# A stack of graph and expert layers on one core: late rotations folded inside the batch rounds, with rows made by GpSimd

## The chip, the cores and the metric

The kernel runs on one core of one Trainium2 chip. The metric is device time in microseconds (us) of one execution. A core has TensorE (PE; its weight loads stand apart as PEld), VectorE (DVE), ScalarE (ACT), GpSimd (POOL), SyncE (SP), which here only issues transfers, and 16 DMA engines that all queues share. Each engine works off its own instructions in order, and the engines meet at semaphores.

## What is computed

Eight layers follow one another on 6250 nodes of 256 values, with 100,000 edges. The change lies in the first. It builds a 256x256 matrix from plane rotations, one an edge, applied in the order of the edges, and multiplies the normalised nodes by it:

```python
def _build_mat(rots, idx_i, idx_j, ndim):
    def step(mat, t):
        i, j, theta = t
        c, s = jnp.cos(theta), jnp.sin(theta)
        ri, rj = mat[i], mat[j]
        mat = mat.at[i].set(c * ri - s * rj)
        mat = mat.at[j].set(s * ri + c * rj)
        return (mat, None)
    mat, _ = jax.lax.scan(step, jnp.eye(ndim), (idx_i, idx_j, rots))
    return mat.T
...
x = x + _layernorm(x) @ _build_mat(edge_weight, src, dst, 256)
```

The rotation's i is the edge's source and j its destination. The edges are sorted by destination and their numbers run to 6249, while the matrix has 256 rows; a read past the end gives the last row, a write past it does nothing.

## The kernel before

The kernel is a row of phases. A phase (`Phase`) holds a block with one program for each engine and ends when all engines have come to its end. The first phases are `constants`, `rotations`, `layernorm_stats` and `x_plus_product`, and the expert layer follows.

`constants` makes an identity and a row of column numbers, and SyncE loads the whole of x into `g.x`; the phase ends when x is in.

`rotations` builds the matrix `m`. An edge whose destination is below 256 is *early*: it changes two rows. An edge whose destination is higher but whose source is below 256 is *late*: it only scales row i and adds a multiple of the last row to it. The phase goes through these steps.

1. SyncE loads sources, destinations and weights. DVE counts the early edges, prepares their event records, and POOL scatters the records to DRAM (`steps`) with 40 indirect DMAs. Then SyncE writes a padding behind them (L2911).
2. DVE makes a record for each late edge (`rec`, stored by ScalarE as `late_records`) and lists, for each of 128 partitions, the late edges it holds (`keys`, then `edge`), in passes of eight. At L3138 the list is done.
3. The batches (L3147 to L3175). 64 events make a batch. SyncE loads a batch's events (`own`, `around`); DVE works out which event feeds which (L3151 to L3166) and releases the load of the next batch; TensorE squares that matrix six times (`powers`), with a copy by ScalarE between; at each of the six levels DVE adds TensorE's product `p_t` to `t` (L3170). TensorE then turns `t` and multiplies it by `m` (ScalarE copies twice), and DVE updates `m` (L3173, L3174).
4. POOL fetches, while the batches run, the late records of each partition's list: it copies 56 indices (L2957) and issues 56 indirect DMAs (L2961), each of which brings one record of four numbers to each partition (`got`).
5. The folds (L3179 to L3187). DVE takes the records one after another. For each it makes two one-hot rows of 256 (L3183, L3184: column number equal to the source, times a factor), and folds them into the pair `ab` with two more instructions (L3185, L3186).
6. The tail. TensorE turns `ab`, DVE multiplies the partitions' pairs together and applies them to `m`, and TensorE turns the result into `g.mt`.
7. ScalarE, at the end of its program, issues 21 large writes that fill and clear tables of later layers (`inject8`, `inject4`, and in `clear_first` `expert_rows` and `back`); the first expert layer waits for them by `g.filled`.

`layernorm_stats` then has DVE go over the 49 tiles of x for mean and variance, and `x_plus_product` starts with ScalarE's normalising of the first tile.

All four numbers that set the loops (blocks of early edges, batches, units of late edges, events) are counted by the kernel in `sizes` and loaded into registers. No planner is at work: the order on each engine is the order of the code.

## Time and profile before

| | us |
|---|---|
| median of 3 runs | 8275.56 (8267.13 to 8279.29) |
| profiled execution, its time | 8263.3 |
| its span, first to last instruction | 8261.1 |
| busy in the span: PE, DVE, ACT, POOL | 5259.0, 3680.5, 3299.8, 4671.5 |

The profile is of one execution, and times in its rows count from the start of the span. A row of a timeline gives start, duration, engine, line, operation, output and inputs, and in brackets how long the engine stood idle before it and what released it. "q" behind an engine's name means its instruction queue: there it is the time of issuing a DMA. Lines in rows of before are lines of the kernel before.

### The profile page before, as it was taken

What the parts mean: (1) busy time and instruction counts of PE and PEld (TensorE: products, weight loads), DVE (VectorE), ACT (ScalarE), POOL (GpSimd) and SP (SyncE); (2) the same over time, 40 slices, a digit from 0 to 9 for tenths busy, and PEclk for the clock granted to TensorE, in tenths of its full rate; (3) what the DMA queues carried; (4) which work ended last, traced back from release to release, by engine and by line L of the source; (5) the groups of instructions that cost most, each with busy time, mean ns of one, the idle gap of its engine ahead of it and who ended that gap; (6) DMA issues with size and microseconds to landing.
All of it is one profiled execution on the core that took longest, in us unless ns stands there. A gap on an engine that the chain in (4) does not pass through costs nothing. (4 is left out here: it accounts for less than half of the span.)

```text
span 8261.1 us, 93318 instructions
## 1 busy us (share of the span) xinstructions
PE 5259.0 (64%) x20514; PEld 3953.8 (48%) x20515; DVE 3680.5 (45%) x8680; ACT 3299.8 (40%) x7876; POOL 4671.5 (57%) x4904
## 2 busy tenths in 40 slices
PE   2259956777635555679744434477677577777896
PEld 2156634555434444456544333355455355555664
DVE  5644446777740000364420000366666566666544
ACT  0043234444344433345443333244443444444453
POOL 5021337777537777314337777577775677773243
PEclk9669977666767777769855555577777777777798
DMA  1142224444323333131211111233443334442213
GB/s 59 50 165 69 65 76 116 117 116 116 108 68 104 104 104 104 53 107 64 91 39 26 26 26 26 63 110 110 110 110 97 92 110 111 111 111 77 97 62 131
DMA packets 395127, 723.28 MB, mean 88 GB/s; under 512 B 117204, under 2 KB 252470, under 8 KB 391602
## 3 DMA queue, kind: packets, MB, share of 16 engines
q0 software_dynamic: 210544, 509.17, 22.1%
q1 hardware_dynamic: 174598, 170.65, 6.6%
q10 hardware_dynamic: 9532, 39.01, 1.2%
q14 instruction: 364, 2.98, 0.1%
q8 instruction: 89, 1.46, 0.1%
HBM read 600.76 MB, written 123.53 MB: 88 GB/s over the span
## 5 line engine op out<-in xcount | busy, mean ns | idle before, releaser
L776 POOL DMA_INDIRECT g_rows<-table,src_idx x2352 | 2233.1, 949 | 717.3 <-issue 717.3
L1051 PE MATMUL g_p_win<-g_rows,g_hot 128*128 128x264 f32 (+1 forms) x4704 | 1545.5, 488 | 44.5 <-issue 41.6
L1051 PEld LDWEIGHTS g_p_win<-g_rows,g_hot 128*128 128x128 f32 x4704 | 1100.8, 245 | 316.9 <-issue 93.8
L941 ACT ACTIVATE g_hot<-iota,near 128x128 f32<-128x128 f32 x2352 | 720.0, 386 | 461.1 <-PE g_p_win L1051 415.8
L776 POOL DMA_INDIRECT g2p_rows<-rows,src_idx x784 | 749.4, 956 | 239.0 <-issue 239.0
L776 POOL DMA_INDIRECT gcnp_rows<-table,src_idx x784 | 748.3, 954 | 239.2 <-issue 239.2
L857 DVE TENSOR_TENSOR g_rows<-g_rows,g_p_w 128x1792 f32<-128x1792 f32 x336 | 679.0, 2021 | 31.3 <-DVE g_carry L817 5.6
L960 ACT ACTIVATE g_resets_f<-fwd_reset 128x112 f32 (+3 forms) x168 | 54.8, 326 | 1151.9 <-DVE g_b L828 1042.4
L1008 PE MATMUL g_p_turn<-slide,g_a 128*8 128x128 f32 (+1 forms) x168 | 61.9, 368 | 700.8 <-DVE g_a L816 700.8
L864 DVE TENSOR_TENSOR agg<-agg,g2p_p_out 128x256 f32 x112 | 42.1, 417 | 960.2 <-PE g2p_p_out L1013 960.2
L1051 PE MATMUL g2p_p_win<-g2p_rows,g2p_hot 128*128 128x256 f32 x1568 | 424.3, 437 | 54.3 <-DMA g2p_rows<-rows,src_idx 54.3
L864 DVE TENSOR_TENSOR agg<-agg,gcnp_p_out 128x64 f32 x112 | 20.3, 221 | 974.0 <-PE gcnp_p_out L1013 973.7
L2609 POOL DMA_INDIRECT back<-e_y,goes x210 | 213.3, 1016 | 399.6 <-DVE e_y L2689 394.8
L1013 PE MATMUL gcnp_p_out<-gcnp_win,gcnp_moved 128*128 128x64 f32 x224 | 62.0, 433 | 580.9 <-DMA gcnp_rows<-table,src_idx 580.6
L1051 PEld LDWEIGHTS g2p_p_win<-g2p_rows,g2p_hot 128*128 128x128 f32 x1568 | 360.8, 230 | 123.9 <-issue 54.7
L1013 PE MATMUL g2p_p_out<-g2p_win,g2p_moved 128*128 128x256 f32 x224 | 114.8, 667 | 454.2 <-DMA g2p_rows<-rows,src_idx 453.7
L2637 PE MATMUL e_p_h<-agg,e_xt 128*128 x840 | 399.4, 598 | 0.0
L2651 PE MATMUL e_p_y<-e_w2s,e_ht 128*128 x1680 | 397.1, 380 | 0.0
L2605 POOL DMA_INDIRECT e_xin<-rows,token x210 | 205.2, 977 | 310.2 <-SPq L2595 242.5
L1051 PE MATMUL gcnp_p_win<-gcnp_rows,gcnp_hot 128*128 128x64 f32 x1568 | 346.2, 421 | 22.9 <-DMA gcnp_rows<-table,src_idx 22.9
L1008 PEld LDWEIGHTS g_p_turn<-slide,g_a 128*8 128x8 f32 (+1 forms) x168 | 14.8, 88 | 712.2 <-issue 712.2
L945 ACT ACTIVATE g_hot<-g_hot,ones 128x896 f32<-128x896 f32 x336 | 350.0, 1042 | 11.0
(797 smaller groups left out, 10976.8 us busy)
## 6 DMA issues: line engine op xcount, KB each, us to landing
g_rows<-table,src_idx POOLq DMA_INDIRECT x2352
c_row<-back SPq DMA_DIRECT2D x35, 896.0 KB, 7.9
back<-agg ACTq DMA_DIRECT2D x7, 1792.0 KB, 34.2
g_inj<-inject SPq DMA_DIRECT2D x56, 224.0 KB
g2p_rows<-rows,src_idx POOLq DMA_INDIRECT x784
rows<-r_row SPq DMA_DIRECT2D x98, 128.0 KB, 3.2
gcnp_rows<-table,src_idx POOLq DMA_INDIRECT x784
table<-agg SPq DMA_DIRECT2D x24, 520.0 KB, 3.1
```

The source lines that it names most:

```text
L776: gp.indirect_dma_start(rows[:, s, j, 0:width + H], None, table, bass.IndirectOffsetOnAxis(g.src_idx[:, at:at + 1], 0)).then_inc(got[s], 16)
L857: V.tensor_tensor(x, x, weight[:, js, :].unsqueeze(3).to_broadcast([P, HALF, H, C]), ALU.mult).then_inc(weighed, 1)
L864: V.tensor_tensor(into, into, p_out[k][:, 0:W], ALU.add).then_inc(added, 1)
L941: last = nc.scalar.activation(hot[:, j, :], g.iota[:, :], ACT.Square, scale=-1.0, bias=g.near[:, bass.ds(c * J + j, 1)])
L945: nc.scalar.activation(ones, ones, ACT.Relu, scale=-1.0, bias=g.ones[:, 0:1]).then_inc(halves, 1)
L1008: nc.tensor.transpose(out, src, g.ident[0:rows_in, 0:rows_in]).then_inc(turned, 1)
L1013: last = nc.tensor.matmul(p_out[k][:, 0:W], moved[:, s % 2, k * P:(k + 1) * P], win[:, :], start=True, stop=True)
L1051: last = nc.tensor.matmul(p_win[:, 0:W], hot[:, j, :], rows[:, s, j, :], start=(j == 0), stop=(j == J - 1))
L2605: gp.indirect_dma_start(xin[:, i % AHEAD, :], None, g.rows, bass.IndirectOffsetOnAxis(g.token[:, i:i + 1], 0)).then_inc(x_in[i % AHEAD], 16)
L2609: gp.indirect_dma_start(g.back, bass.IndirectOffsetOnAxis(g.goes[:, i:i + 1], 0), y[:, i % AHEAD, :], None, bounds_check=BACK - 1, oob_is_ ...
L2637: last = nc.tensor.matmul(p_h[s % 2][:, :], xt[:, s % 2, k, :], w1s[:, of(at), k * F:(k + 1) * F].rearrange("p a f -> p (a f)"), start=(k ...
L2651: last = nc.tensor.matmul(p_y[s % 2][:, :], ht[:, s % 2, b, :], w2s[:, of(at), b * D:(b + 1) * D].rearrange("p a f -> p (a f)"), start=(b ...
```

## The change

- `constants` no longer loads x. SyncE loads it in `rotations`, behind the padding write.
- The statistics of x (`Norms`) are made in `rotations`: DVE goes over the 49 tiles when its list is done, and `layernorm_stats` is no longer called there.
- Batches and folds are one loop of *rounds*. A round is a batch and a group of `LG` = 8 folds; there are as many rounds as the larger of batches and groups. Past the last batch SyncE would load the padding, past the last group POOL fetches an inert record.
- In a round POOL fetches eight records and then makes the 16 one-hot rows itself (`hots`). DVE keeps the two folding instructions, which stand between the levels: folds 0 and 1 ahead of the first level, 2, 3 and 4 ahead of the third to fifth, 5 to 7 behind the last.
- POOL makes row pair k of a round when DVE has folded pair k of the round before (`ao`); DVE waits for each pair (`hot`).
- The 21 clearing writes are issued by SyncE behind its loop of batch loads.

```diff
@@ rotations, SyncE
                 sp.dma_start(g.steps[bass.ds(total, UB), :], inert[:, :]).then_inc(padded, 16)
+                sp.dma_start(g.x[:, 0:NT - 1, :], g.x_dram[0:(NT - 1) * P, :].rearrange("(t p) d -> p t d", p=P)).then_inc(x_in, 16)
+                sp.dma_start(g.x[0:LAST, NT - 1, :], g.x_dram[(NT - 1) * P:N_NODES, :]).then_inc(x_in, 16)
                 sp.wait_ge(padded, 16)
                 sp.wait_ge(early_listed, 1)
-                n = sp.value_load(sizes[0:1, 1:2], min_val=0, max_val=NBATCH)
+                sp.wait_ge(sized, 3)
+                n = sp.value_load(sizes[0:1, 5:6], min_val=0, max_val=NBATCH)
...
+                for inject, parts in ((g.inject8, 4), (g.inject4, 2)):
+                    for q in range(parts):
+                        sp.dma_start(inject.rearrange("(p r) q -> p (r q)", p=P)[:, q * cols:(q + 1) * cols], low).then_inc(g.filled, 16)
+                g.fills = 6 + clear_first(sp, g, zero, g.filled)
@@ rotations, GpSimd
-                    G.tensor_copy(ids[:, :], edge[:, bass.ds(i * LU, LU)]).then_inc(ids_ready, 1)
+                    G.tensor_copy(ids[:, :], edge[:, bass.ds(q * LG, LG)]).then_inc(ids_ready, 1)
...
-                    for k in range(LU):
+                    for k in range(LG):
                         gp.indirect_dma_start(got[:, k, :], None, g.late_records, bass.IndirectOffsetOnAxis(ids[:, k:k + 1], 0)).then_inc(fetched, 16)
-                    gp.wait_ge(fetched, 16 * LU * (i + 1))
+                    gp.wait_ge(fetched, 16 * LG * (b + 1))
+                    gp.nop(nofuse=True)
+                    for k in range(LG):
+                        gp.wait_ge(ao, 2 * LG * b + 2 * k + 2)
+                        gp.nop(nofuse=True)
+                        for a in range(2):
+                            G.tensor_scalar(hots[:, k, a, :], iota[:, :], got[:, k, 2:3], got[:, k, a:a + 1], ALU.is_equal, ALU.mult).then_inc(hot, 1)
+                    gp.wait_ge(hot, 2 * LG * (b + 1))
@@ rotations, VectorE
+                z.do(V.tensor_scalar(per_group[0:1, :], iota[0:1, 0:NGROUP], float(LG), some[0:1, 2:3], ALU.mult, ALU.is_lt))
+                z.do(V.tensor_reduce(out=some[0:1, 5:6], in_=per_group[0:1, :], axis=AX.X, op=ALU.add))
+                z.do(V.tensor_copy(sizes[0:1, 4:5], some[0:1, 5:6]), wait=False)
+                z.do(V.tensor_copy(some[0:1, 4:5], sizes[0:1, 1:2]))
+                z.do(V.tensor_tensor(some[0:1, 4:5], some[0:1, 5:6], some[0:1, 4:5], ALU.max))
+                z.do(V.tensor_copy(sizes[0:1, 5:6], some[0:1, 4:5]))
+                V.sem_inc(sized, 1)
...
+                dv.wait_ge(x_in, 32)
+                for n in range(NT):
+                    norms.tile(n)
+                norms.vector(dv)
...
+                folded_at = {0: (0, 1), 2: (2,), 3: (3,), 4: (4,), LEVELS: (5, 6, 7)}
+                def fold(c, b, k):
+                    dv.wait_ge(hot, 2 * LG * b + 2 * k + 2)
+                    c.do(V.scalar_tensor_tensor(out=ab[:, :, :], in0=hots[:, k, 0, :].unsqueeze(1).to_broadcast([P, 2, D]), scalar=1.0, in1=ab[:, :, :], op0=ALU.add, op1=ALU.mult))
+                    c.do(V.tensor_tensor(ab[:, 1, :], ab[:, 1, :], hots[:, k, 1, :], ALU.add))
...
                     for k in range(LEVELS):
+                        for n in folded_at.get(k, ()):
+                            fold(folds, b, n)
                         dv.wait_ge(applied, LEVELS * b + k + 1)
                         s.do(V.tensor_tensor(t[:, :], t[:, :], p_t[:, 0:D], ALU.add))
+                    for n in folded_at[LEVELS]:
+                        fold(folds, b, n)
```

Three places in the order of the instructions; where `rot_` stands ahead of a name it is a buffer of this phase, `agg` holds `hots`, `low` and `zero`.

POOL, the loop of the gathers, before:

```order
L2957 COPY rot_ids<-rot_edge 128x56
L2961 DMA rot_got<-late_records,rot_ids 128x4 x56
L2962 REGISTER_ALU
L2954 REGISTER_ALU
L2954 COMPARE_AND_BRANCH
```

POOL, the same place now, to the second pair of rows; six more pairs like it follow:

```order
L2971 COPY rot_ids<-rot_edge 128x8
L2972 REGISTER_ALU
L2975 DMA rot_got<-late_records,rot_ids 128x4 x8
L2976 REGISTER_ALU
L2979 ISA
L2982 TENSOR_SCALAR agg<-rot_iota,rot_got 128x256 x2
L2979 REGISTER_ALU
L2982 TENSOR_SCALAR agg<-rot_iota,rot_got 128x256 x2
```

Behind each eight gathers POOL now has sixteen row-makings and a wait ahead of each pair.

DVE, one fold in its own loop, before:

```order
L3183 TENSOR_SCALAR rot_f<-rot_iota,rot_got 128x256
L3184 TENSOR_SCALAR rot_oh<-rot_iota,rot_got 128x256
L69 REGISTER_ALU
L3185 SCALAR_TENSOR_TENSOR rot_ab<-rot_f,rot_ab 128x512
L69 REGISTER_ALU
L3186 TENSOR_TENSOR rot_ab<-rot_ab,rot_oh 128x256
```

DVE, inside a round now, from its second fold to the third level:

```order
L3184 SCALAR_TENSOR_TENSOR rot_ab<-agg,rot_ab 128x512
L69 REGISTER_ALU
L3185 TENSOR_TENSOR rot_ab<-rot_ab,agg 128x256
L69 REGISTER_ALU
L3212 ISA
L3213 TENSOR_TENSOR rot_t<-rot_t,rot_p_t 128x256
L69 REGISTER_ALU
L3212 REGISTER_ALU
L3213 TENSOR_TENSOR rot_t<-rot_t,rot_p_t 128x256
L69 REGISTER_ALU
L3183 REGISTER_ALU
L3184 SCALAR_TENSOR_TENSOR rot_ab<-agg,rot_ab 128x512
```

A fold is two instructions now and stands between the levels (L3213), behind a wait for POOL's rows (L3183).

ScalarE, the end of its program in this phase, before:

```order
L3237 ACTIVATE rot_ab_t<-rot_p_tt 128x512
L3242 DMA inject<-agg 128x3136 x6
L2255 DMA expert_rows<-agg 128x2080 x8
L2259 DMA back<-agg 128x3584 x7
L2895 UNCONDITIONAL_BRANCH
```

SyncE, from the last load of a batch to the end of the phase, now:

```order
L2923 DMA rot_around<-steps 128x1024
L2916 REGISTER_ALU
L2916 COMPARE_AND_BRANCH
L2930 DMA inject<-agg 128x3136 x6
L2248 DMA expert_rows<-agg 128x2080 x8
L2252 DMA back<-agg 128x3584 x7
L2892 UNCONDITIONAL_BRANCH
```

The 21 writes moved from ScalarE, behind its copy in the tail, to SyncE, behind its loop of batch loads.

## Rows read from the trace of the kernel before

**Rows 1.** Busy by stretch: us, PE, PEld, DVE, ACT, POOL (instructions), clock, DMA, GB/s

```profile
116.90:280.90 164.00, 103.40 (x432) 72.90 (x432) 79.33 (x224) 24.52 (x64) 51.59 (x53) 0.85 0.09 23
280.90:390.50 109.60, 0.00 (x0) 0.00 (x0) 103.66 (x224) 0.00 (x0) 0.00 (x0) 0.51 0.00 0
398.70:430.20 31.50, 0.00 (x0) 0.00 (x0) 0.03 (x1) 0.00 (x0) 0.00 (x0) 0.50 1.01 424
```

**Rows 2.** Timeline: end of the first phase, first instruction of the rotations

```profile
2.15 0.23 DVE L121 CAST iota<-const_iota_i 128x128 f32<-128x128 int32 x1 [1.00 <-POOL const_iota_i L115]
...
23.53 0.14 POOL L2926 IOTA rot_block_i<- 1x20 int32 x1 [21.42 <-POOLq L46]
```

**Rows 3.** Timeline: padding write, POOL's first gather, DVE's first batch

```profile
55.89 0.58 SPq L2911 DMA_DIRECT2D steps<-rot_inert  x1
...
112.01 0.23 POOL L2957 COPY rot_ids<-rot_edge 128x56 int32 x1 [2.48 <-issue]
...
113.06 1.00 POOL L2961 DMA_INDIRECT rot_got<-late_records,rot_ids  x1 [0.81 <-POOL rot_ids L2957]
...
116.88 0.80 DVE L3151 TENSOR_SCALAR rot_sel<-rot_around,rot_own 128x128 f32<-128x128 f32 x3 [19.77 <-DMA rot_around<-steps]
```

**Rows 4.** Timeline of DVE: the second batch, to the start of the third

```profile
137.64 0.80 DVE L3151 TENSOR_SCALAR rot_sel<-rot_around,rot_own 128x128 f32<-128x128 f32 x3 [0.63 <-DVE rot_m L3174]
...
146.36 0.42 DVE L3170 TENSOR_TENSOR rot_t<-rot_t,rot_p_t 128x256 f32<-128x256 f32 x1 [2.06 <-PE rot_p_t L3281]
...
147.57 0.42 DVE L3170 TENSOR_TENSOR rot_t<-rot_t,rot_p_t 128x256 f32<-128x256 f32 x1 [0.79 <-PE rot_p_t L3281]
...
156.15 0.16 DVE L3173 TENSOR_SCALAR rot_keep<-rot_p_m 128x1 f32<-128x1 f32 x1 [3.31 <-PE rot_p_m L3292]
...
158.20 0.80 DVE L3151 TENSOR_SCALAR rot_sel<-rot_around,rot_own 128x128 f32<-128x128 f32 x3 [0.57 <-DVE rot_m L3174]
```

**Rows 5.** Timeline of DVE: two instructions of the first fold, then the second

```profile
281.71 0.69 DVE L3185 SCALAR_TENSOR_TENSOR rot_ab<-rot_f,rot_ab 128x512 f32<-128x512 f32 x1
282.44 0.42 DVE L3186 TENSOR_TENSOR rot_ab<-rot_ab,rot_oh 128x256 f32<-128x256 f32 x1
282.90 0.41 DVE L3183 TENSOR_SCALAR rot_f<-rot_iota,rot_got 128x256 f32<-128x256 f32 x1
```

**Rows 6.** Group by line, POOL's gathers: busy, mean ns | idle before them

```profile
L2961 POOL DMA_INDIRECT rot_got<-late_records,rot_ids x56 | 54.5, 974 | 17.6 <-issue 16.8 <-POOL rot_ids L2957 0.8
```

**Rows 7.** Timeline: ScalarE's last writes, the statistics, the product's first activation

```profile
410.83 19.36 ACTq L2259 DMA_DIRECT2D back<-agg  x7
...
431.72 16.10 DVE L424 BATCH_NORM_STATS2 ln_n_stats<-x  x49 [32.99 <-PEq L46]
...
450.43 0.21 DVE L441 SCALAR_TENSOR_TENSOR shift<-ln_n_mean,rstd 128x49 f32<-128x49 f32 x1
451.70 0.60 ACT L467 ACTIVATE l0g_xn<-x,shift,rstd 128x256 f32<-128x256 f32 x1 [1.87 <-PEq L519]
```

**Rows 8.** Groups by line and shape on POOL: two inputs, and one

```profile
L1196 POOL TENSOR_TENSOR x<-x,l1f_wide 128x256 f32 x48 | 34.8, 729 | 136.4 <-ACT l1f_xn L467 135.7
...
L113 POOL TENSOR_SCALAR_AFFINE_SELECT slide<-slide 128x384 f32<-128x384 f32 x1 | 0.5, 496 | 0.1
...
L2935 POOL TENSOR_SCALAR_AFFINE_SELECT rot_tri<-rot_tri 128x128 f32<-128x128 f32 x1 | 0.3, 292 | 0.1
```

**Rows 9.** Timeline: two-input operations on POOL and DVE, a later layer

```profile
6383.86 1.90 POOL L1418 TENSOR_TENSOR n_own<-n_own,n_total 128x1024 f32<-128x1024 f32 x1 [1.77 <-DMA n_own<-table]
...
6384.66 2.18 DVE L1553 TENSOR_TENSOR agg<-agg,n_inv 128x1024 f32<-128x1024 f32 x1
...
6387.96 1.20 DVE L1553 TENSOR_TENSOR agg<-agg,n_inv 128x1024 f32<-128x1024 f32 x1
```

**Rows 10.** DMA issues: KB each, median us from issue to landing

```profile
back<-agg ACTq DMA_DIRECT2D x7, 1792.0 KB, 34.2
...
back<-e_y,e_idx POOLq DMA_INDIRECT x8, 3.4
```

More of the change, by code:

```diff
@@ L2798 @@
 NUNIT = -(-TP // LU)
+LG = 8
+NGROUP = NUNIT * LU // LG
 VAR = 8
@@ L2866, in rotations @@
         ab = ph.sb("ab", [P, 2, D])
-        f, oh = [ph.sb(f"f{s}", [P, D]) for s in range(2)], [ph.sb(f"oh{s}", [P, D]) for s in range(2)]
         ab_t, scan_a, scan_b = ph.sb("ab_t", [P, 2, 2, P]), ph.sb("scan_a", [P, 2, P]), ph.sb("scan_b", [P, 2, P])
@@ L2884, in rotations @@
             ph.sem(n) for n in ("lo", "l_waves", "l_sq", "l_counted", "l_summed", "l_products", "l_turned", "rec_made", "rec_stored", "listed"))
[L2885 removed]
+        drawn, ids_ready, fetched, hot = (ph.sem(n) for n in ("drawn", "ids_ready", "fetched", "hot"))
         batch_in, batch_read, so, squared, powered, applied, t_turn, t_copied, x_made, x_copied, spread = (
@@ L3139, in _ @@
                 V.sem_inc(listed, 1)
+                dv.wait_ge(x_in, 32)
+                for n in range(NT):
+                    norms.tile(n)
+                norms.vector(dv)
                 dv.nop(nofuse=True)
-                batches = dv.value_load(sizes[0:1, 1:2], min_val=0, max_val=NBATCH)
+                rounds = dv.value_load(sizes[0:1, 5:6], min_val=0, max_val=NBATCH)
+                V.sem_inc(ao, 2 * LG)
+                folded_at = {0: (0, 1), 2: (2,), 3: (3,), 4: (4,), LEVELS: (5, 6, 7)}
+                assert sorted(sum(folded_at.values(), ())) == list(range(LG))
                 writers = around[:, :, :].rearrange("p e (k f) -> p f k e", k=2)[:, 6, :, :]
@@ L3175, in _ @@
                     assert s.n == PER_S, s.n
-                dv.nop(nofuse=True)
-                with dv.Fori(0, units) as i:
-                    dv.wait_ge(fetched, 16 * LU * (i + 1))
-                    s = Chain(dv, ao, 4 * LU * i)
-                    for k in range(LU):
-                        one, other = f[k % 2], oh[k % 2]
-                        s.do(V.tensor_scalar(one[:, :], iota[:, :], got[:, k, 2:3], got[:, k, 0:1], ALU.is_equal, ALU.mult), wait=False)
-                        s.do(V.tensor_scalar(other[:, :], iota[:, :], got[:, k, 2:3], got[:, k, 1:2], ALU.is_equal, ALU.mult))
-                        s.do(V.scalar_tensor_tensor(out=ab[:, :, :], in0=one[:, :].unsqueeze(1).to_broadcast([P, 2, D]), scalar=1.0, in1=ab[:, :, :], op0=ALU.add, op1=ALU.mult))
-                        s.do(V.tensor_tensor(ab[:, 1, :], ab[:, 1, :], other[:, :], ALU.add))
-                    V.sem_inc(eaten, 1)
                 V.sem_inc(ab_ready, 1)
```

58 lines of the change are left out of this document (29 added, 29 removed).

## The prediction

> **What bounds the kernel now.** I read the busy times by stretch first, then the timeline of the first 460 us, engine by engine. The change touches only the stretch from the start to the first activation of the product that follows the rotations, which begins at 451.70 us [rows 7]; everything behind it is the same program. So the whole forecast is one question: when does that activation start afterwards?
>
> The stretch is a row of pieces that hardly overlap. To 23.53 us no engine of the rotations has begun, because the first phase ends only when x has arrived [rows 2]. Then the edges are sorted into early and late. VectorE (DVE) is done with its lists at 116.88 - 19.77 = 97.1 us and sits idle 19.77 us until the first batch of early events has landed [rows 3]. From 116.9 to 280.9 us run the batches, 164 us with DVE busy 79 us [rows 1]; ScalarE runs 64 instructions there, 6 levels and 2 copies a batch, so there are 8 batches. From 280.9 to 390.5 us DVE alone folds the late edges, 103.7 us busy, with every other engine at zero [rows 1]. The gathers for these folds lie inside the batches on GpSimd (POOL), 56 of them [rows 6]. A tail ends at 431.72 - 32.99 = 398.7 us, and then DVE waits to 431.72 us [rows 7]: ScalarE is still issuing the clearing writes until 410.83 + 19.36 = 430.2 us while the DMA engines are full [rows 1, 7]. Last come the layernorm statistics, 431.72 to 450.64 us.
>
> **The change, part by part.** I lay out the new time axis point by point.
>
> *x's load out of the first phase.* The last instruction there is then DVE's cast, over at 2.38 us [rows 2]. From a phase's last issue to the next phase's first instruction the trace shows 430.19 to 431.72, 1.5 us [rows 7]. So the rotations begin near 4.1 instead of 23.5 us: 19.4 us earlier. The load now stands on SyncE's queue behind the padding write, in front of the batch loads. That write was issued at 55.89 us, now near 37 [rows 3]; the load took under 23.5 us before, and DVE needs it at 79, so some 18 us of slack cover it. It also shares the DMA engines with POOL's scatters, whose completion is wanted only at about 92. I cost this at nothing.
>
> *Statistics into DVE's gap.* DVE finishes its lists at 97.1 - 19.4 = 77.7 us, plus six new one-row instructions at about 0.2 (the 128x1 one in rows 4 takes 0.16), 78.9. The statistics need 450.64 - 431.72 = 18.9 us [rows 7], to 97.8; with one register load more, about 98.8. The first batch has landed by 116.88 - 19.4 = 97.5. So the gap swallows them but for 1.3 us. ScalarE waits for the variance in front of its loop, and has nothing to do there before that.
>
> *Clearing writes from ScalarE's end to SyncE's.* SyncE issues the last batch's load in the seventh round and then the 21 writes, whose issue took 38 us before. That lies beside the last one and a half rounds, so the 31.5 us between 398.7 and 430.2 go. What is queued behind: the eighth round's gathers on POOL meet full DMA engines. Writes of this kind land after a median of 34.2 us, and indirect writes among other traffic after 3.4 [rows 10]. This can cost 0 to 34 us, once. A small gather is nearer to the second row; I take 4.
>
> *Folds in the rounds.* Rounds are the larger of batches (8) and groups of eight folds (at most 56 / 8 = 7): 8 rounds with 64 folds. DVE keeps two of the four instructions of a fold, 281.71 to 282.90, 1.19 us [rows 5]. In a batch of 158.20 - 137.64 = 20.56 us DVE has waits of 2.06 before the first level, 0.79 before a later one, and 3.31 at the end [rows 4]. Folds 0 and 1 overrun the first by 2.38 - 2.06 = 0.32, folds 2 to 4 overrun 0.79 by 0.40 each, folds 5 to 7 overrun 3.31 by 0.26: a round bound by DVE and TensorE is 20.56 + 1.8 = 22.3 us.
>
> *POOL's round.* It copies indices and starts the first gather 1.05 us later, and after its last indirect DMA it took 2.48 us to go on [rows 3]; eight gathers cost (54.5 + 17.6) / 56 = 1.29 us each, 10.3 [rows 6]. That is 13.9 us in which it makes no one-hot row. Then it makes 16 of them, 128x256, one tensor in, two operations with per-partition scalars. The trace has none. POOL's select with one input takes 0.50 us at 384 and 0.29 at 128 columns, so 0.39 at 256; its two-input operation at 128x256 takes 0.73 [rows 8]. These are my ends; with two operations and two scalars to fetch I take the middle, 0.56: 9.0 us. Without any interference POOL's round is 22.9, about as long as DVE's.
>
> *Interference.* A POOL operation with two inputs began at 6383.86 and ran 1.90 us; DVE's two-input operation, 1.20 us when alone, began at 6384.66 and took 2.18, so it ended 1.08 us after POOL's end [rows 9]. The two excluded each other. Both fold instructions read two tensors in SBUF, 1.11 us busy together (0.69 and 0.42), and they become ready just when POOL makes the next rows. Ends: no fold displaces POOL (0), or all eight do (8.9). Folds 0, 1 and 5 to 7 stand in bunches and run straight off POOL's rows, while folds 2 to 4 wait for levels; I take five of eight, 5.6 us. Round: 13.9 + 9.0 + 5.6 = 28.5 us, bound by POOL.
>
> *Sum.* POOL starts its first round at 112.01 - 19.4 + 0.4 for a second register load = 93.0. Eight rounds, 228.0; the last fold and the last two updates, 2.6; the delayed gathers, 4; the tail, 398.7 - 390.5 = 8.2; the change of phase, 1.5. The product starts at 337.3 instead of 451.7: 114 us sooner. The profiled execution took 8263.3 us, so 8149; the median of the runs shown lies 12.3 above it, so I forecast 8275.6 - 114 = 8161 us. TensorE's clock, 0.85 of full in the batches [rows 1], may fall in a longer round; what that adds lies beside POOL's work, and I cost it at nothing.
>
> **Rivals.** *The chain bounds.* If one-hot rows are cheap or do not collide, a round is 22.3. DVE starts at 98.8, waits some 2.5 us for the first rows, and the product starts at 98.8 + 2.5 + 178.4 + 9.7 = 289.4: 162 us sooner, 8113. For it: the exclusion is shown for POOL with two inputs, and these have one. Against it: POOL's fetch leaves only 8.4 us for 16 rows.
> As an estimate from the Trainium skill, GPSIMD Engine Reference, section 3.1, which gives 1.03 cycles an element at 1.2 GHz for a body of at most two operations, sixteen rows would cost 3.5 us and their dispatch, and the round 23.0 even with the collisions above, a saving of 158 us; no run here shows that rate with two scalars.
>
> *Every fold excludes POOL, or rows are dear.* At 0.56 with all eight a round is 13.9 + 9.0 + 8.9 = 31.8, the product starts at 363.7 and the time is 8188; at 0.73, 34.5, 385.3 and 8209. For it: the exclusion in rows 9 was complete.
> This is what the Trainium skill says, SBUF — State Buffer, section Who interferes with whom: a DVE instruction with two SBUF inputs contends with any GpSimd instruction that reads SBUF, and the later one blocks fully. It speaks against handing these rows to POOL; rows 9 agree for a two-input POOL operation, with 2.18 us in place of 1.20, and no row shows a one-input one.
>
> *Slower than before: the one-hot rows cost more than the folds did.* The start stays at 451.7 when 109.3 + 8 rounds reach it, that is at 42.8 us a round: 20 us for 16 rows behind fetch and exclusion, 1.25 us a row, 1.7 times the two-input price. At 1.4 us a round is 45.2 and the kernel 19 us slower, 8295. Nothing in rows 8 is that dear.
>
> *The moves do not do what they say.* If x came late, or the clearing writes held SyncE past the rounds, 20 to 30 us of the gain would be lost. The slack above speaks against both.
>
> **How the numbers follow.** Round of 25 to 31 us: 0.47. Bound by the chain, under 25: 0.25. Exclusion or dear rows, 31 to 40: 0.20. Near 43: 0.03. Above 45: 0.05. The forecast is the first, 8161. The range runs from the chain's 8113, less 5 for a faster restart, to a round of 36 us, 8222: 8108 to 8222. It leaves out the end of the dear case and the last two. About 0.2%, 16.5 us, is what a measurement can tell from no change, so faster 0.92, same 0.03, slower 0.05.
>
> **What would show it.** In the changed profile: POOL's first instruction of the rotations near 4 us; DVE's 49 statistics ending near 98 and no separate statistics phase; rounds of 28 us counted by DVE's first line of a round; DVE's waits in them released by POOL's one-hot rows, at 0.4 to 0.7 us each; DVE's fold instructions well over 0.69 and 0.42, or POOL's rows uneven, if they exclude each other; the last gathers landing late; no idle stretch behind the tail. A round near 22 us with DVE waiting for TensorE alone, or one over 31, makes the forecast wrong.

## The result

The changed kernel takes 8221.5 us (median of 4 runs, 8217.1 to 8223.4) where the kernel before, beside it on the same chip, took 8277.4: a ratio of 0.9933, with a 95% interval of 0.9916 to 0.995. That is 56 us less. The direction was right, the size was half of the forecast 114. The time lies at the upper end of the forecast's range (8108 to 8222), which stood for a round of 36 us.

The time axis first. The timeline of the changed kernel, several engines, with the start, the duration and in brackets the idle time before and what ended it:

```profile
3.10 0.14 POOL L2936 IOTA rot_block_i<- 1x20 int32 x1 [0.97 <-POOLq L46]
...
77.52 16.11 DVE L417 BATCH_NORM_STATS2 rot_n_stats<-x 128x6 f32<-128x256 f32 x49
...
98.46 0.90 DVE L3192 TENSOR_SCALAR rot_sel<-rot_around,rot_own 128x128 f32<-128x128 f32 x3 [1.98 <-DMA rot_around<-steps]
...
319.18 6.17 SPq L2930 DMA_DIRECT2D inject<-agg  x6
...
342.35 17.65 SPq L2252 DMA_DIRECT2D back<-agg  x7
...
394.87 1.09 ACT L460 ACTIVATE l0g_xn<-x,shift,rstd 128x256 f32<-128x256 f32 x2 [7.65 <-PEq L512]
```

Each line answers to one of before. The rotations begin at 3.10 us instead of 23.53 [rows 2]. The statistics stand in what was DVE's idle time, and the first batch begins at 98.46 instead of 116.88 [rows 3]. The clearing writes are issued from 319 to 360 us, inside the rounds, and no idle stretch follows the tail. The product's first activation stands at 394.87 instead of 451.70 [rows 7]: 56.8 us earlier, which is the whole gain between the medians. (The two profiled executions as wholes lie 45.9 us apart, 8261.1 and 8215.2: behind the product the same program took 9.8 us longer in the second, less than the 15 us by which single runs of the kernel before differ.) Up to the first batch 18.4 of the 56.8 were won, so from there on the changed kernel needs 296.4 us and the one before 334.8.

One round of GpSimd, from the copy of its indices to the next copy:

```profile
164.57 0.21 POOL L2971 COPY rot_ids<-rot_edge 128x8 int32 x1 [0.57 <-POOL agg L2982]
165.53 1.04 POOL L2975 DMA_INDIRECT rot_got<-late_records,rot_ids  x1 [0.76 <-POOL rot_ids L2971]
...
178.29 21.73 POOL L2982 TENSOR_SCALAR agg<-rot_iota,rot_got 128x256 f32<-128x256 f32 x16 [2.46 <-DMA rot_got<-late_records,rot_ids]
200.59 0.21 POOL L2971 COPY rot_ids<-rot_edge 128x8 int32 x1 [0.57 <-POOL agg L2982]
```

This round is 36.0 us, the mean from the second copy to the eighth is 35.8: 13.7 from the copy to the first row, as forecast (13.9), and then 21.7 for 16 one-hot rows, where the forecast had 9.0 and 5.6 for collisions. The groups by line of the rounds (98 to 390 us; busy, mean ns | idle time before and its main releaser), then one line for all rows (ns, shortest/median/longest), and below them who waited for whom on DVE (total us, times, longest), last that of the kernel before:

```profile
L2982 POOL TENSOR_SCALAR agg<-rot_iota,rot_got 128x256 f32<-128x256 f32 x128 | 171.1, 1348 | 23.8 <-DMA rot_got<-late_records,rot_ids 23.8
...
L3184 DVE SCALAR_TENSOR_TENSOR rot_ab<-agg,rot_ab 128x512 f32<-128x512 f32 x64 | 50.8, 794 | 90.2 <-POOL agg L2982 86.1
L3185 DVE TENSOR_TENSOR rot_ab<-rot_ab,agg 128x256 f32<-128x256 f32 x64 | 32.6, 510 | 2.2
```

```profile
L2982 POOL TENSOR_SCALAR agg<-rot_iota,rot_got x128: 1210/1228/1755, 106.4 to 381.2; 128x256 f32<-128x256 f32 x128
```

```profile
DVE rot_ab L3184 <- POOL agg L2982: 86.1, 31, 10.7
DVE rot_t L3213 <- PE rot_p_t L3309: 18.4, 16, 1.3
...
DVE rot_t L3170 <- PE rot_p_t L3281: 48.7, 48, 2.3
```

A row takes 1.35 us on the mean. DVE sits 86 us waiting for rows, and where it waited 48.7 us for TensorE's levels before, two of the 48 times in [rows 4], it now waits 18.4. GpSimd itself waits only for its fetches to land (23.8 us), never for DVE. So GpSimd bounds the rounds, as forecast, but with rows at more than twice the price.

### The profile page after: what moved, and what is told of

The parts are those of the page before. It is cut to its first block and busy times, and to the rows that moved or that the text cites. A ratio compares the mean times of both kernels' runs of the same rounds, so it can differ in the third digit from the quotient of the medians.

```text
span 8215.2 us, 93454 instructions
## 1 busy us (share of the span) xinstructions
PE 5253.9 (64%) x20514; PEld 3945.3 (48%) x20515; DVE 3664.7 (45%) x8590; ACT 3302.1 (40%) x7876; POOL 4867.4 (59%) x5047
## 3 DMA queue, kind: packets, MB, share of 16 engines
q0 software_dynamic: 210800, 509.19, 22.3%
## 5 line engine op out<-in xcount | busy, mean ns | idle before, releaser
L1044 PE MATMUL g_p_win<-g_rows,g_hot 128*128 128x264 f32 (+1 forms) x4704 | 1517.5, 480 | 44.0 <-issue 40.9
L1044 PEld LDWEIGHTS g_p_win<-g_rows,g_hot 128*128 128x128 f32 x4704 | 1078.5, 240 | 308.3 <-issue 90.9
```

The costliest lines, as they stand in the source:

```text
L1044: last = nc.tensor.matmul(p_win[:, 0:W], hot[:, j, :], rows[:, s, j, :], start=(j == 0), stop=(j == J - 1))
```

## The experiments

The kernel before ran beside each group of kernels; its median lay between 8267.4 and 8278.8 us from group to group, and not all groups ran on the same chip, so kernels of different groups are compared by their ratio to it and by the start of the product's first activation in the trace (451.7 before, 394.9 changed).

**A row by itself.** Instructions added to the kernel before on GpSimd, one at a time. Those behind the wait for `ao` run while VectorE (DVE) is in its folds, those behind the wait for `fo` when the folds are over:

```diff
+row = lambda n=D: G.tensor_scalar(pr[:, 0:n], iota[:, 0:n], pc[:, 0:1], pc[:, 1:2], ALU.is_equal, ALU.mult)
+gp.wait_ge(ao, 4 * 4)
+for _ in range(20):
+    probe(row())
...
+gp.wait_ge(fo, 13)
+for _ in range(2):
+    probe(row())
...
```

> The kernel before, with instructions added on GpSimd that nothing uses: 20 rows of the changed kernel's form (TENSOR_SCALAR of 128x256, equal to a per-partition scalar, then times a per-partition scalar), one after the other while VectorE works through its late folds; 20 MEMSETs of 128x256 in the same loop; and, after the last fold, when VectorE has little to do, two each of: the row, the row at 128 columns, the row with two constants in place of the scalars, the comparison alone, the product alone, a product and sum with constants, and a TENSOR_TENSOR product. Theory A, the row is dear by its form, whatever else runs: the quiet row takes 1.15 to 1.25 us, as the lowest of the changed kernel (1.21), and beside the folds 1.25 to 1.4. Theory B, the row itself is near 0.55 us as forecast, and VectorE's folds keep GpSimd out for the rest: the quiet row 0.4 to 0.75 us, beside the folds 1.2 or more. Within A: if the per-partition scalars are dear, the row with constants falls to 0.5 to 0.7; if the comparison is, the product alone does; if it is the second operation, each single operation takes about half of 1.2. The time of the whole run may be up to some 15 us above the kernel before and says nothing here.

The groups of GpSimd by line and shape, first those beside the folds, then those after them (busy us, mean ns of one | idle time before):

```profile
L2973 POOL TENSOR_SCALAR rot_pr<-rot_iota,rot_pc 128x256 f32<-128x256 f32 x20 | 28.1, 1407 | 106.4 <-DVE rot_ab L3218 104.5
...
L2973 POOL TENSOR_SCALAR rot_pr<-rot_iota,rot_pc 128x256 f32<-128x256 f32 x2 | 2.4, 1222 | 44.0 <-DVE mt L3238 43.9
L2986 POOL TENSOR_SCALAR rot_pr<-rot_iota 128x256 f32<-128x256 f32 x2 | 2.1, 1069 | 0.2
L2990 POOL TENSOR_SCALAR rot_pr<-rot_iota,rot_pc 128x256 f32<-128x256 f32 x2 | 1.9, 927 | 0.2
L2988 POOL TENSOR_SCALAR rot_pr<-rot_iota,rot_pc 128x256 f32<-128x256 f32 x2 | 1.8, 922 | 0.2
L2973 POOL TENSOR_SCALAR rot_pr<-rot_iota,rot_pc 128x128 f32<-128x128 f32 x2 | 1.6, 794 | 0.2
L2994 POOL TENSOR_TENSOR rot_pr<-rot_iota 128x256 f32<-128x256 f32 x2 | 1.2, 613 | 0.2
L2992 POOL TENSOR_SCALAR rot_pr<-rot_iota 128x256 f32<-128x256 f32 x2 | 0.8, 408 | 0.2
```

Theory A: with nothing beside it the row takes 1.22 us, and beside VectorE's folds 1.41. Collisions are worth 0.1 to 0.2 us a row on the mean; the price itself is the row's. None of the three readings inside theory A came true: with constants in place of the scalars (L2986) the row still takes 1.07 us, and the comparison (L2988) or the product (L2990) alone takes 0.92, neither little nor half. But a product and sum with constants (the last line) takes a third of the row.

**What makes the row dear.** A second set of forms in the same quiet place:

> The kernel before, with two each of eight GpSimd instructions of 128x256 added after the last fold, that nothing uses: the row (compare, multiply, both with per-partition scalars), the comparison with a constant alone, the product with a constant alone, comparison and sum with constants, product and sum with two per-partition scalars, difference and product with two per-partition scalars, and TENSOR_TENSOR difference and product with a broadcast column. The first probe gave 1.22 us for the row, 1.07 with constants, 0.92 for either operation alone with a scalar, 0.41 for product and sum with constants. If the price lies in reading scalars (0.5 us for the first, 0.3 for the second), product and sum with two scalars take 1.2, and the comparison with a constant 0.4 or somewhat more. If it lies in the comparison, product and sum with two scalars stay at 0.9 or less, and the comparison with a constant takes 0.9 or more. The TENSOR_TENSOR forms are expected at 0.61, as the product of the first probe. The time of the whole run says nothing here.

In the order of the list: product and sum with scalars is L2984, difference and product with scalars L2986, the comparison with a constant L2978, the product with a constant L2980, comparison and sum with constants L2982, and the TENSOR_TENSOR forms L2988 and L2990:

```profile
L2986 POOL TENSOR_SCALAR rot_pr<-rot_iota,rot_pc 128x256 f32<-128x256 f32 x2 | 2.5, 1227 | 0.2
L2982 POOL TENSOR_SCALAR rot_pr<-rot_iota 128x256 f32<-128x256 f32 x2 | 2.2, 1076 | 0.2
L2980 POOL TENSOR_SCALAR rot_pr<-rot_iota 128x256 f32<-128x256 f32 x2 | 1.7, 852 | 0.2
L2978 POOL TENSOR_SCALAR rot_pr<-rot_iota 128x256 f32<-128x256 f32 x2 | 1.7, 850 | 0.2
L2988 POOL TENSOR_TENSOR rot_pr<-rot_iota,rot_pc 128x256 f32<-128x256 f32 x2 | 1.2, 614 | 0.2
L2990 POOL TENSOR_TENSOR rot_pr<-rot_iota,rot_pc 128x256 f32<-128x256 f32 x2 | 1.2, 614 | 0.2
...
L2984 POOL TENSOR_SCALAR rot_pr<-rot_iota,rot_pc 128x256 f32<-128x256 f32 x2 | 1.1, 558 | 0.2
```

Neither of my two readings holds. The comparison alone costs as much as the product alone, 0.85 us, so it is not the comparison. Product and sum with two scalars takes 0.56, so it is not the scalars either: they add 0.07 for one and 0.15 for two. Of the forms tried, product-and-sum is the only cheap TENSOR_SCALAR; every other, even a lone product, is 0.85 us or more, and a second operation adds 0.2 to 0.3. A lone product costs twice a product with a sum. Why is not settled by these runs.

**The rows made cheap.** The same kernel with the cheap form in the rows' place, on scalars that are zero, so that the late folds are left out of the result:

```diff
-G.tensor_scalar(hots[:, k, a, :], iota[:, :], got[:, k, 2:3], got[:, k, a:a + 1], ALU.is_equal, ALU.mult).then_inc(hot, 1)
+G.tensor_scalar(hots[:, k, a, :], iota[:, :], nil[:, 0:1], nil[:, 1:2], ALU.mult, ALU.add).then_inc(hot, 1)
...
+V.memset(nil[:, :], 0.0).then_inc(nil_made, 1)
```

> The changed kernel with each row made by product and sum with two per-partition scalars that are zero, in place of comparison and product: same tiles, shapes and count, 0.56 us alone instead of 1.22 (measured after the folds). The late folds are left out of the result by this; nothing else is changed. It asks whether the price of the row was the only step of the forecast that was wrong. Theory A, it was: GpSimd's round is 35.8 less 16 x (1.34 - 0.65) = 24.8 us at 0.56 and some 0.1 for folds that keep it out, or VectorE's own sum of 22.3 to 25; the product's first activation near 394.9 - 88 = 307 us, the kernel near 8131 us where the changed kernel takes 8219. Theory B, cheaper rows meet VectorE's folds more often and are kept out for whole folds as I had priced it (5.6 us a round): 28 to 29 us a round, 8162 us. Theory C, something else holds the round: over 31 us, 8185 us or more.

8134.0 us, ratio 0.9839 (0.9822 to 0.9855), the first activation at 321.4. So with rows at the price I had assumed the gain is 1.6%, 133 us on 8277, more than the 114 forecast: the row's price accounts for the whole shortfall. (Of the gain over the changed kernel some 6 us are landings, which fall from 23.8 us in all to 17.9.) Against the changed kernel (0.9925 to 0.9933) it is 71 to 78 us, between theory A's 88 and B's 57, and the way there is not quite that of either. The group of the rows, DVE's wait for them, and some of DVE's batch instructions in one round; the last line is the second of them in the changed kernel, where GpSimd is still fetching at that time:

```profile
L2984 POOL TENSOR_SCALAR agg<-rot_iota,rot_nil 128x256 f32<-128x256 f32 x128 | 86.5, 688 | 17.9 <-DMA rot_got<-late_records,rot_ids 17.9
```

```profile
DVE rot_ab L3187 <- POOL agg L2984: 2.9, 2, 2.4
```

```profile
209.80 0.36 DVE L3198 TENSOR_SCALAR rot_last<-rot_last 128x3 f32<-128x3 f32 x1
...
210.68 0.43 DVE L3200 SCALAR_TENSOR_TENSOR rot_none<-rot_last,rot_own 128x3 f32<-128x3 f32 x1
211.14 0.90 DVE L3201 TENSOR_TENSOR rot_coefs<-rot_coefs,rot_own 128x384 f32<-128x384 f32 x1
...
134.12 0.15 DVE L3197 SCALAR_TENSOR_TENSOR rot_none<-rot_last,rot_own 128x3 f32<-128x3 f32 x1
```

GpSimd's round falls to 24.5 us and runs ahead; DVE hardly waits for rows (2.9 us in all) and sets a round of 26.2 (154.24 to 285.21 in five rounds). Its batch instructions now stand beside the rows and stretch: 0.36, 0.43 and 0.90 us for what takes 0.19, 0.15 and 0.56 in the changed kernel. So the collision is real, and both sides pay: on the mean 0.13 us a row on GpSimd (0.69 against 0.56), and 0.17 to 0.34 on each of these three instructions of DVE.

**The moves alone.** Batches, then folds, rows by DVE, as before; only the load, the statistics and the clearing writes moved:

```diff
 sp.dma_start(g.steps[bass.ds(total, UB), :], inert[:, :]).then_inc(padded, 16)
+sp.dma_start(g.x[:, 0:NT - 1, :], g.x_dram[0:(NT - 1) * P, :].rearrange("(t p) d -> p t d", p=P)).then_inc(x_in, 16)
+sp.dma_start(g.x[0:LAST, NT - 1, :], g.x_dram[(NT - 1) * P:N_NODES, :]).then_inc(x_in, 16)
...
 V.sem_inc(listed, 1)
+dv.wait_ge(x_in, 32)
+for n in range(NT):
+    norms.tile(n)
+norms.vector(dv)
...
-ac.wait_ge(fill_ready, 2)
+sp.wait_ge(fill_ready, 2)
```

> The kernel before with the three moves alone (x's load behind the lists' loads, the statistics behind the lists, the clearing writes on SP's queue behind the batches' loads); batches and then late folds stay as they were, the folds' rows made by VectorE. Theory A, the rounds lose time and the moves win more than the whole gain: VectorE's first batch begins at 98.5 us as in the changed kernel, batches 164 and folds 110 us follow as in the kernel before, and the product's first activation is near 381.5 us instead of 451.7: 70 us less than before, some 8207 us, 13 us faster than the changed kernel. Theory B, the rounds win part of it: the first activation comes after 394.9 us, and the kernel takes more than 8222 us.

Theory A. 8197.2 us beside 8267.8 for the kernel before, ratio 0.9915 (0.9901 to 0.9928), and in the timeline:

```profile
380.59 1.09 ACT L460 ACTIVATE l0g_xn<-x,shift,rstd 128x256 f32<-128x256 f32 x2 [7.64 <-PEq L512]
```

The moves win 71.1 us; the changed kernel as a whole 56.8. To see that this is no difference of the chip, the changed kernel ran again with the next group:

> The changed kernel once more, beside the others of this chip and their run of the kernel before: on the first chip it took 0.9933 of the kernel before. The kernel with the moves alone took 0.9915 beside its own run of before. If the rounds really lose some 14 us against batches and folds apart, this one comes out at 0.993 again, near 8212 us if the kernel before takes 8268; if the two chips differ in this, at 0.9915 or less (8197).

8218.6 us, ratio 0.9925 (0.9909 to 0.9942), first activation at 393.9. The intervals of 0.9915 and 0.9925 overlap, so the whole times don't rank the two; the first activations in the traces do, 380.6 against 393.9 and 394.9.

**The rounds alone.** The changed kernel with the three moves undone:

```diff
-dv.wait_ge(x_in, 32)
-for n in range(NT):
-    norms.tile(n)
-norms.vector(dv)
...
+ac.wait_ge(fill_ready, 2)
...
 rotations(nc, g)
+layernorm_stats(nc, g)
```

> The changed kernel with the three moves undone (x's load waited for ahead of the rotations, the statistics in a stage of their own after them, the clearing writes on the queue of ScalarE behind them); the rounds with GpSimd's rows stay. Theory A, the rounds cost 14 us and the moves bring 71: the rounds begin at about 117 us, take 8 x 35.8 = 287 where batches and folds took 273.6, the rest as before: 13 us more than the kernel before, ratio 1.0016, 8281 us if that takes 8268. Theory B, the rounds are long only because the moves stand beside them (the clearing writes run during the last two rounds): the rounds fall under 33 us, and the kernel takes 10 us or more less than before, under 8258 us.

8278.2 us against 8278.8, ratio 0.9998 (0.9988 to 1.0008); first activation at 453.5, 1.8 us later than before. The rounds by themselves win nothing and lose nothing that can be measured: less than the 13 us that theory A had. They are 34.5 us here, not under the 33 of theory B. Moves and rounds added up give -71.1 + 1.8 = -69.3, together they give -56.8: 12.5 us go where both stand together. The traces show where. GpSimd's last gather, its rows and SyncE's load of the next batch, in the rounds alone:

```profile
193.55 0.94 POOL L2972 DMA_INDIRECT rot_got<-late_records,rot_ids  x1 [0.30 <-issue]
...
194.60 0.54 SPq L2927 DMA_DIRECT2D rot_around<-steps  x1
...
196.06 4.18 POOL L2979 TENSOR_SCALAR agg<-rot_iota,rot_got 128x256 f32<-128x256 f32 x3 [1.56 <-DMA rot_got<-late_records,rot_ids]
```

and in the changed kernel, where the last gather of the round runs from 174.89 to 175.83:

```profile
174.89 0.94 POOL L2975 DMA_INDIRECT rot_got<-late_records,rot_ids  x1 [0.30 <-issue]
...
175.34 0.53 SPq L2923 DMA_DIRECT2D rot_around<-steps  x1
```

With the rounds alone the broadcast load of 512 KB goes out 0.1 us behind the last gather's end (194.49), in the changed kernel 0.5 us ahead of it; the landing takes 2.46 us in place of 1.56. Over all rounds GpSimd's rows wait 23.8 us for landings here and 13.2 with the rounds alone, and the 64 gathers take 65.2 us against 63.0: 12.8 us, about the loss. 4.6 of them are the last round's landing, 6.16 us, beside the clearing writes.

**The load held back.** Whether the order of the load and the last gather is what lengthens the landing, a wait ahead of the batch loads tells:

```diff
 sp.wait_ge(batch_read, b + 1)
+sp.wait_ge(ao, 2 * LG * b + 2)
```

> The changed kernel with one wait added on SP's queue: a batch's load is issued only when the first fold of the round before it is done, some 8 us later than now and after GpSimd's last fetch of that round. With the moves, the broadcast load (512 KB) goes out at 175.34, during the last of 8 gathers (174.89 to 175.83), and the rows wait 2.46 us for the fetches to land; without the moves it goes out 0.1 us behind the last gather, and they wait 1.6. Theory A, the load ahead of the last gather's packets delays them by 0.9 us in each round: the landing falls to 1.6 us, the round from 35.8 to 34.7, 8 us less in all, some 8211 us where the changed kernel takes 8219; the last round keeps its landing of some 6 us behind the clearing writes. Theory B, the landing is longer for another reason: it stays at 2.5 us and the time within 3 us of 8219.

```profile
209.52 4.18 POOL L2983 TENSOR_SCALAR agg<-rot_iota,rot_got 128x256 f32<-128x256 f32 x3 [1.65 <-DMA rot_got<-late_records,rot_ids]
```

Theory A: the landing is 1.57 to 1.77 us in all rounds but the last (6.01), the round 34.7 us, the first activation at 386.6, 8.3 earlier, although my wait held back the first load too (the first batch begins at 102.7, which GpSimd's rounds hide). The wait holds back all three loads of a batch; but the two small ones go out ahead of the last gather's end in the rounds alone as well (193.36 and 194.02), and the landing there is 1.56, which points to the broadcast load. In the total it gives 8211.4 us, ratio 0.992 (0.9903 to 0.9936), which overlaps the changed kernel's intervals: the mechanism is shown by the trace, the gain in the whole time is not resolved.

**Fewer rows.** 7 folds in a round instead of 8; there are 8 rounds either way.

```diff
-LG = 8
+LG = 7
-folded_at = {0: (0, 1), 2: (2,), 3: (3,), 4: (4,), LEVELS: (5, 6, 7)}
+folded_at = {0: (0, 1), 2: (2,), 3: (3,), 4: (4,), LEVELS: (5, 6)}
```

> The changed kernel with 7 late folds in a round instead of 8 (8 rounds still, since 51 is the most late edges that a partition has; 5 folds fewer over dead slots in all, the two last of a round behind the levels instead of three). Theory A, GpSimd's chain of fetches and rows sets the round: each round loses one gather, 1.29 us (its row and the idle time before it), and two rows, 2.7 us: 35.8 becomes 31.8, the 8 rounds 32 us less, 8189 us. Theory B, the chain of VectorE and TensorE sets it: a round loses one fold of VectorE, 1.3 us and a part of its wait, 8 rounds 10 us, 8211 us.

8167.8 us, ratio 0.9879 (0.9864 to 0.9894), first activation at 354.0. GpSimd's round, from copy to copy:

```profile
123.22 0.19 POOL L2971 COPY rot_ids<-rot_edge 128x7 int32 x1 [0.59 <-POOL agg L2982]
...
153.60 0.20 POOL L2971 COPY rot_ids<-rot_edge 128x7 int32 x1 [0.57 <-POOL agg L2982]
```

30.4 us, 5.4 less, where 4.0 were expected: two rows and a gather, and the landing fell to 1.7, the load now going out behind the last gather here too. By the ratios that is some 41 us off the changed kernel, where 32 were expected. Theory A in its direction: two rows taken from GpSimd are two rows off the round, though DVE loses only one fold; most of the rest of the 5.4 is the shorter landing, 0.9.

**The rows back on DVE.**

```diff
-        G.tensor_scalar(hots[:, k, a, :], iota[:, :], got[:, k, 2:3], got[:, k, a:a + 1], ALU.is_equal, ALU.mult).then_inc(hot, 1)
-gp.wait_ge(hot, 2 * LG * (b + 1))
+gp.wait_ge(taken, b + 1)
...
+V.tensor_copy(held[:, :, :], got[:, :, :]).then_inc(taken, 1)
+c.do(V.tensor_scalar(one[:, :], iota[:, :], held[:, k, 2:3], held[:, k, 0:1], ALU.is_equal, ALU.mult), wait=False)
+c.do(V.tensor_scalar(other[:, :], iota[:, :], held[:, k, 2:3], held[:, k, 1:2], ALU.is_equal, ALU.mult))
```

> The changed kernel with the rows made by VectorE again (0.33 us each and 0.4 for the second, as in the kernel before), from a copy of what GpSimd fetched, so that GpSimd only fetches, one round ahead; the rounds and the moves stay. Theory A, GpSimd's rows set the round: a round falls from 35.8 to about 28.5 us (the batch of 20.6, 8 folds of about 2 us each less the waits on TensorE that they fill), the product's first activation comes near 338 us, 8164 us in all. Theory B, the round is long because of the folds in the batch's gaps whoever makes the rows: it stays above 33 us, the kernel above 8200 us.

8166.5 us, ratio 0.9881 (0.9866 to 0.9896), first activation at 352.2. Two batches' first instructions on DVE:

```profile
191.04 0.80 DVE L3194 TENSOR_SCALAR rot_sel<-rot_around,rot_own 128x128 f32<-128x128 f32 x3 [0.52 <-DVE rot_m L3221]
...
221.67 0.80 DVE L3194 TENSOR_SCALAR rot_sel<-rot_around,rot_own 128x128 f32<-128x128 f32 x3 [0.52 <-DVE rot_m L3221]
```

A round of 30.6 us, under theory B's 33 but above the 28.5 that I had: 8 folds of 1.95 and 15.0 for the batch. I had let the folds fill the batch's waits on TensorE whole; at two of the six levels a wait of 1.2 to 1.3 us is left. Rounds with the rows on DVE beat rounds with the rows on GpSimd by 43 us.

**The rows divided.** 7 folds a round, GpSimd makes the second row of each fold, DVE the first:

```diff
-for a in range(2):
-    G.tensor_scalar(hots[:, k, a, :], iota[:, :], got[:, k, 2:3], got[:, k, a:a + 1], ALU.is_equal, ALU.mult).then_inc(hot, 1)
+G.tensor_scalar(hots[:, k, :], iota[:, :], got[:, k, 2:3], got[:, k, 1:2], ALU.is_equal, ALU.mult).then_inc(hot, 1)
...
+c.do(V.tensor_scalar(one[:, :], iota[:, :], held[:, k, 2:3], held[:, k, 0:1], ALU.is_equal, ALU.mult))
```

> 7 folds in a round, and of a fold's two rows GpSimd makes the second and VectorE the first (from a copy of what was fetched). GpSimd's round: 12.1 us of copy, fetch and landing and 7 rows of 1.31 = 21.3 us. VectorE's: 15.0 us for the batch with its remaining waits (30.6 less 8 folds of 1.95, from the kernel whose rows VectorE makes) and 7 folds of 0.41 + 0.72 + 0.46 = 1.6, 26.2 us. Theory A, a round is the longer of the two engines' own sums: 26 to 27 us, 8 rounds 31 us less than with 7 folds and both rows on GpSimd (30.4 a round, 8168 us): 8137 us. Theory B, the two engines hinder each other at their rows and folds by more than the 0.1 to 0.2 us a row seen so far: a round of 29 us or more, 8155 us or more.

8155.7 us, ratio 0.9848 (0.9832 to 0.9865), first activation at 331.8: ahead of the kernel before and of the changed one, and the fastest here but for the one that leaves the folds out. From 7 folds with both rows on GpSimd it is 0.31% by the ratios, 26 us, whose intervals just touch, and 22 us by the first activations, where 31 were expected. That lies between the two theories. All rows on DVE with 7 folds a round was not run; from 30.6 us with 8 folds of 1.95 I estimate 28.7 us a round for it, so against that the division is worth little. GpSimd's copies, and what DVE waited for:

```profile
190.98 0.67 POOL L2972 COPY rot_ids<-rot_edge 128x7 int32 x1 [6.83 <-DVE rot_held L3186]
...
218.63 0.67 POOL L2972 COPY rot_ids<-rot_edge 128x7 int32 x1 [6.76 <-DVE rot_held L3186]
```

```profile
DVE rot_t L3220 <- PE rot_p_t L3316: 16.8, 16, 1.3
DVE rot_keep L3225 <- PE rot_p_m L3327: 11.1, 14, 1.6
```

The round is 27.7 us between these two copies and 28.0 on the mean, by DVE's first instruction from the second round on: 1.5 to 1.8 over DVE's own sum of 26.2. Waits on TensorE come back at the batch's end (L3225) as the folds get shorter. GpSimd now waits 6.8 us a round for DVE. Whether those can be used was the last question: both rows of the folds 0, 1, 5 and 6 on GpSimd.

```diff
-G.tensor_scalar(hots[:, k, :], iota[:, :], got[:, k, 2:3], got[:, k, 1:2], ALU.is_equal, ALU.mult).then_inc(hot, 1)
+for a in ((0, 1) if k in BOTH else (1,)):
+    G.tensor_scalar(hots[:, ROW_AT[k] - 1 + a, :], iota[:, :], got[:, k, 2:3], got[:, k, a:a + 1], ALU.is_equal, ALU.mult).then_inc(hot, 1)
```

> The kernel with 7 folds a round and the rows divided, with four more rows moved from VectorE to GpSimd (both rows of the folds 0, 1, 5 and 6, which stand ahead of and behind the levels; of the folds 2 to 4, whose length hides the waits on TensorE, VectorE keeps the first row). GpSimd had 6.8 us of idle time in a round of 27.65; four rows of 1.3 leave 1.6. VectorE sheds four rows of 0.45: 1.8. Theory A, the round is VectorE's sum: 25.9 us, 8 rounds 14 us less, 8142 us where the divided kernel took 8156. Theory B, what VectorE sheds turns into waits on TensorE or on rows that come late (the two engines' sums are then within 0.3 us of each other): the round stays above 27 us, 8150 us or more.

8162.5 us, ratio 0.9859 (0.9843 to 0.9876), first activation at 334.7: no better.

```profile
DVE rot_keep L3234 <- PE rot_p_m L3336: 20.6, 15, 2.5
...
DVE rot_ab L3199 <- POOL agg L2987: 3.0, 2, 1.9
```

Theory B: what DVE shed it now waits for TensorE, 20.6 us in place of 11.1 at the batch's end, and the mean round, counted as above, is 28.0 in both. The 2.9 us by which the first activation comes later arise in the first round, whose rows are late.

## Why the prediction was right or wrong

**The moves: right.** By the prediction's own terms the moves without the rounds give 98.8 + 273.6 + 8.2 + 1.5 = 382.1 for the first activation; the run gave 380.6. Point by point in the changed kernel: rotations from 3.10 (forecast 4.1), first batch at 98.46 (98.8), GpSimd's first copy at 93.5 (93.0), the last gathers' landing 6.16, 3.6 over the mean of the other seven (4), and no idle stretch for the clearing writes.

**GpSimd as the bound of the rounds: right.** DVE waited 86 us for rows. Fetch and landing were 14.3 us with the step back to the copy (13.9). There luck helped: the 2.48 us that I took for the landing was idle time behind other DMAs, and the landing came to 2.5 only because of the batch load beside it; undisturbed it is 1.6.

**The price of a row: wrong, and it is the step that failed.** "These are my ends; with two operations and two scalars to fetch I take the middle, 0.56: 9.0 us", between 0.39 and 0.73 from [rows 8]. A row is 1.22 us alone, 1.35 in place. The ends were rows of other forms, one of them an instruction with two tensors, and I took the instruction with one tensor to lie below. The second probe shows why that bound was none: TENSOR_TENSOR takes 0.61 us in the quiet place, TENSOR_SCALAR anything from 0.41 to 1.23 by its pair of operations. 0.56 happens to be the measured price of product and sum with two scalars; mine was comparison and product. A round came to 35.8 us instead of 28.5, and 8 x 7.3 = 58 us is the distance between 114 and 56.8. By terms: the row's own price adds 16 x 0.66 = 10.6 us, collisions take off 3.6 (below), fetch and landing add 0.4. By the prediction's own sign, a round over 31, its forecast is wrong.

A sentence of the prediction had it cheaper still: as an estimate by the rate in the Trainium skill, GPSIMD Engine Reference, section 3.1, 1.03 cycles an element at 1.2 GHz, sixteen rows would cost 3.5 us and their dispatch. The rounds show 21.7 us for them. The first probe leaves dispatch aside: its row took 0.79 us at 128 columns and 1.22 at 256, so 128 columns cost 0.43 us, 3.3 ns each, where that rate makes 0.86. The measurement decides: that rate is not one to price these rows by.

**The collisions: real, and mis-sized.** I had 5.6 us a round on GpSimd. Measured are 0.13 us a row on the mean (1.35 against 1.22), 2.0 us a round; with cheap rows again 0.13. The mean hides that the rows differ: the median is 1.23, which is the quiet price, and the longest takes 1.76 (the line of all rows above). Had I known the row at 1.22 and kept the 5.6, the forecast would have been a round of 13.9 + 19.5 + 5.6 = 39.0, and a gain of 30 us: the two errors had opposite signs. My evidence, [rows 9], was one pair of 128x1024 operations of which one waited for the other's end. Here a fold's instruction beside a row took up to 1.05 us in place of 0.69, 0.36 more, far less than a row's length. The Trainium skill, SBUF — State Buffer, section Who interferes with whom, says that a DVE instruction with two SBUF inputs contends with GpSimd's reads; the trace agrees in that the fold's first instruction went from 0.69 us [rows 5] to 0.79 on the mean (L3184 above), but shows no block for the length of a whole row.

**The rival "the chain bounds", 22.3 us a round: not reached, and its round was too short.** With cheap rows DVE set the round, at 26.2. In the five rounds from 154.24 us of that kernel DVE is busy 105.9 of 131.0 us, 21.2 a round, where the batch before had 10.0 (the first line below) and eight folds of 1.19 make 19.5: 1.7 us are DVE's instructions stretching beside the rows. It waits 10.6 us for TensorE there, 2.1 a round, 0.5 more than the two waits of 0.79 that the forecast left. The rest, by subtraction some 1.7 us, is time between DVE's own instructions, of which a round now has more; I had not counted it.

TensorE is also slower in a longer round. One batch's 54 matmuls before and in the changed kernel, by stretch (us, PE, PEld, DVE, ACT, POOL busy, mean granted clock, DMA, GB/s):

```profile
137.60:158.20 20.60, 12.98 (x54) 9.12 (x54) 10.02 (x29) 3.06 (x8) 15.73 (x17) 0.83 0.12 27
...
131.40:167.20 35.80, 17.07 (x54) 12.10 (x54) 20.37 (x44) 3.07 (x8) 29.71 (x26) 0.60 0.06 15
```

The clock has two levels in these stretches, 0.5 and 1.0 of full (1.2 and 2.4 GHz). In the second one, read in slices, it is at 0.50 from 143.4 to 155.4 us, after TensorE's last matmul had ended at 140.6, and at 1.00 from 156.4 to 159.4, after TensorE had been busy from 151.4 to 155.4. I had costed the clock at nothing because GpSimd bounds. For the changed kernel that held (DVE waits for rows, not for levels). For the divided rows, where waits on TensorE are what is left, it need not hold; what the clock costs there was not taken apart.

**The rival "every fold excludes POOL, or rows are dear", 31 to 40 us a round: what came, by its second half.** I gave it 0.20. The rows were dear, at more than the 0.73 that it went up to, and its full exclusion did not come, so its 34.5 us a round lie near the measured 35.8 by luck. (The range's end, 8222 for a round of 36, is 8221 by the prediction's own sum.)

**The rival "slower than before" by dear rows: its mechanism came, its point didn't.** I put the point at 42.8 us a round, a row at 1.25 us with full exclusion, 8.9 us a round. The row alone came at 1.22, the exclusion at 2.0, and the round at 35.8.

## What to carry to other kernels

Price an instruction on GpSimd by a row of the same operation pair, not by its shape or its count of inputs; if the trace has none, the range of the cost was a factor of three here (0.41 to 1.23 us), and so must the forecast's be. When work moves to an idle engine, compare the moved work's own length there with what it saves here: 16 rows cost DVE some 6.5 us a round and GpSimd 21.7, so the idle engine became the bound; half of the rows on each was better than all of them on GpSimd, and all of them on DVE came close. And a change of several parts is worth running part by part: here the moves alone are ahead of the whole, by the first activations in the traces.

## What the runs showed of the hardware that I had not expected

On GpSimd, at 128x256 in fp32, a TENSOR_SCALAR of product and sum takes 0.41 us with constants and 0.56 with two per-partition scalars, a lone product or a lone comparison 0.85, comparison and sum 1.08, difference and product or comparison and product with two scalars 1.22; TENSOR_TENSOR takes 0.61. The same row at 128 columns takes 0.79, so, as an estimate from these two widths, some 0.37 us of it don't depend on the columns (0.79 less 0.43 for 128 of them).

A 512 KB load that is issued 0.5 us ahead of the end of the last of eight small gathers delays their landing from 1.6 to 2.5 us; the same load issued later doesn't. And rows on GpSimd (the cheap ones, in the kernel without late folds) stretch even a DVE instruction of three elements a partition, from 0.15 to 0.43 us.
